# The 16-step loop of the two middle layers, written out with an order of work for each engine

## The reference, cut to what matters

```
def _layer(x, wqkv, qs, ksc, wo, lg, lb, w1, b1, w2, b2):
    h = shift_token(x)                      # second half of the channels comes from the token before
    q, k, v = split(h @ wqkv)               # 8 heads of 64
    q, k = rotary_xpos(l2norm(q) * qs, l2norm(k) * ksc)
    o = local_attention(q, k, v)            # windows of 128: own window and the one before, masked softmax
    x = x + o @ wo
    h = shift_token(x)
    h = (h - mean) / sqrt(var + 1e-5) * lg + lb
    a, g = split(h @ w1 + b1)               # 2 x 682
    return x + (a * gelu(g)) @ w2 + b2
```

## Time and profile before

| what | us |
|---|---|
| median of 3 runs | 3072.92 (3065.40 to 3076.16) |
| the profiled execution, time | 3070.95 |
| its span, first to last instruction | 3069.2 |
| PE busy in the span | 2724.8 (89%) |
| DVE busy | 2044.3 (67%) |
| ACT busy | 1430.0 (47%) |
| POOL busy | 1000.7 (33%) |

### The profile page before, as it was taken

One profiled execution on the slowest core, in us unless ns is written; L12 is line 12 of the kernel. 1 busy time (PEld: TensorE's weight loads), 2 busy tenths in 40 slices (PEclk: granted clock), 3 DMA queues, 4 the chain that ended last, 5 costly groups with the idle time before them and its releaser, 6 DMA issues. The chain is left out here.

```text
span 3069.2 us, 60378 instructions
## 1 busy us (share of the span) xinstructions
PE 2724.8 (89%) x20578; PEld 2415.7 (79%) x20578; DVE 2044.3 (67%) x5302; ACT 1430.0 (47%) x3028; POOL 1000.7 (33%) x906
## 2 busy tenths in 40 slices
PE   7999999958999999997799999999858899679997
PEld 6998898847888888886688888888847688577886
DVE  6777777637777777774577777777647355484554
ACT  5666676624555555553355555555426111062111
POOL 2222222224333333331343333333224333263332
PEclk8999999969999999998799999999979899889998
DMA  1011110022222222222222222222234101041100
GB/s 64 26 31 34 35 34 31 23 92 71 80 64 68 82 63 69 78 67 76 73 73 72 68 75 67 67 80 63 66 108 137 60 28 35 30 132 38 42 28 21
DMA packets 222985, 188.10 MB, mean 61 GB/s; under 512 B 22356, under 2 KB 204504, under 8 KB 221912
## 3 DMA queue, kind: packets, MB, share of 16 engines
q1 hardware_dynamic: 203224, 174.42, 17.7%
q10 hardware_dynamic: 19584, 11.35, 1.2%
HBM read 89.95 MB, written 44.04 MB: 44 GB/s over the span
## 5 line engine op out<-in xcount | busy, mean ns | idle before, releaser
L1292 ACT ACTIVATE b_sb_probs<-b_sb_probs,b_sb_neg_top,b_sb_r_norm 128x256 f32<-128x256 f32 x512 | 265.7, 590 | 155.4 <-DVE b_sb_neg_top L1400 154.4
L1212 POOL TENSOR_TENSOR b_sb_r_norm<-b_sb_squares,b_sb_power 128x8 f32<-128x8 f32 x64 | 105.0, 1641 | 705.6 <-DVE b_sb_squares L1359 705.6
L2166 ACT ACTIVATE c_sb_kern_hi<-c_sb_kern 128x512 fp32r<-128x512 f32 x128 | 80.8, 632 | 428.3 <-DVE c_sb_kern L2186 428.3
L2143 POOL TENSOR_TENSOR c_sb_kern_lo<-c_sb_kern,c_sb_kern_hi 128x512 fp32r<-128x512 f32 x128 | 166.7, 1303 | 312.9 <-ACT c_sb_kern_hi L2166 312.9
L118 PE MATMUL psum<-b_sb_fT_lo,b_sb_w_hi 128*128 128x256 f32 x768 | 229.6, 299 | 27.9 <-DVE b_sb_fT_lo L1462 27.9
L2182 DVE SCALAR_TENSOR_TENSOR c_sb_kern<-psum,cu_bias 128x512 f32<-128x512 f32 x128 | 88.4, 691 | 246.4 <-PE psum L120 246.3
L1393 DVE CUSTOM_DVE_ANT_0 b_sb_probs<-psum,b_sb_mask_now 128x256 f32<-128x256 f32 x512 | 196.6, 421 | 64.5 <-PE psum L1539 57.7
L120 PE MATMUL psum<-b_sb_fT_hi,b_sb_w_hi 128*128 128x256 f32 x768 | 218.5, 285 | 0.0
L119 PE MATMUL psum<-b_sb_fT_hi,b_sb_w_lo 128*128 128x256 f32 x768 | 217.8, 284 | 0.0
L1329 ACT ACTIVATE b_sb_gate<-psum,b_sb_b 128x256 f32<-128x256 f32 x192 | 90.6, 474 | 271.8 <-PE psum L120 271.7
L118 PE MATMUL psum<-c_sb_kern_lo,cu_v_hi 128*128 128x512 f32 x512 | 206.9, 404 | 2.9 <-POOL c_sb_kern_lo L2143 2.9
(11 more groups left out here) (309 smaller groups left out, 9014.1 us busy)
## 6 DMA issues: line engine op xcount, KB each, us to landing
b_sb_v_prev<-b_sb_v_now SPq DMA_DIRECT2D x64, 260.0 KB, 2.3
b_sb_kT_hi<-b_sb_kT_hi SPq DMA_DIRECT2D x64, 256.0 KB, 2.5
b_sb_kT_lo<-b_sb_kT_lo SPq DMA_DIRECT2D x64, 256.0 KB, 2.6
Y<-b_sb_y SPq DMA_DIRECT2D x128, 128.0 KB, 1.7
b_sb_res<-Y SPq DMA_DIRECT2D x64, 128.0 KB, 2.2
b_sb_h_in<-Y ACTq DMA_DIRECT2D x128, 64.0 KB, 1.8
b_sb_x_f<-Y SPq DMA_DIRECT2D x128, 64.0 KB, 1.9
b_sb_res_f<-Y SPq DMA_DIRECT2D x64, 128.0 KB, 2.1
```

Of the source, the lines that this page charges most:

```text
L1212: pool.tensor_tensor(r, s, p, ALU.pow).then_inc(r_ready[b], 1)
L1292: ins = act.activation(probs[b][:, n, :], probs[b][:, n, :], ACT.Exp, bias=neg_top[b][:, n:n + 1], scale=r_norm[b][:, h:h + 1])
L2143: pool.tensor_tensor(kern_lo[n][:], kern[n][:], kern_hi[n][:].bitcast(F32), ALU.subtract)\
```

## The change

The loop of `layer_b` is written out: `staggered`, `Chain`-based waits of the loop and `fence` go, `turns` and `in_turns` come in, as in layer a. Step numbers are then plain integers: all waits and addresses are constants. Its stages compute the same as before.

```
-    order = [("load", 1, 0), ("load_r", 0, -2), ("load_r", 1, -2), ("scores", 1, -1), ("residual", 1, -1),
-             ("project_k", 0, 0), ("scores2", 1, -1), ("turn_p", 1, -1), ("project_q", 0, 0), ("turn_p2", 1, -1),
-             ("turn_f", 0, -2), ("project_v", 0, 0), ("up", 0, -2), ("up", 1, -2), ("mid", 0, -2), ("values", 1, -1),
-             ("up", 2, -2), ("mid", 1, -2), ("turn_h", 1, 0), ("up", 3, -2), ("mid", 2, -2), ("turn_o", 1, -1),
-             ("up", 4, -2), ("mid", 3, -2), ("turn_qk", 0, 0), ("out", 1, -1), ("up", 5, -2), ("mid", 4, -2), ("mid", 5, -2),
-             ("load", 0, 1), ("load_f", 0, -1), ("load_f", 1, -1), ("scores", 0, 0), ("residual", 0, 0),
-             ("project_k", 1, 0), ("scores2", 0, 0), ("down", 0, -2), ("turn_p", 0, 0), ("project_q", 1, 0),
-             ("turn_p2", 0, 0), ("project_v", 1, 0), ("values", 0, 0), ("moments", 0, -1), ("down", 1, -2),
-             ("turn_o", 0, 0), ("norm", 0, -1), ("turn_h", 0, 1), ("turn_qk", 1, 0), ("rope", 0, 1), ("out", 0, 0)]
+    order = {
+        "act": [("turn_f", 0, -4), ("mid", 4, -5), ("project_v", 0, -2), ("turn_o", 1, -3), ("mid", 5, -5), ("up", 0, -4),
+               ("up", 1, -4), ("project_v", 1, -2), ("turn_h", 0, -1), ("load", 1, -1), ("turn_qk", 1, -2),
+               ("scores", 0, -2), ("mid", 0, -4), ("scores2", 0, -2), ("scores", 1, -2), ("mid", 1, -4), ("turn_p2", 0, -2),
+               ("project_k", 0, -1), ("scores2", 1, -2), ("up", 2, -4), ("turn_h", 1, -1), ("up", 3, -4),
+               ("project_q", 0, -1), ("mid", 2, -4), ("turn_p2", 1, -2), ("project_k", 1, -1), ("load", 0, 0), ("up", 4, -4),
+               ("mid", 3, -4), ("turn_o", 0, -2), ("up", 5, -4), ("turn_qk", 0, -1), ("project_q", 1, -1)],
+        "pe": [("scores", 0, -1), ("up", 0, -3), ("up", 1, -3), ("project_v", 1, -1), ("turn_h", 0, 0), ("turn_qk", 1, -1),
+               ("out", 1, -2), ("scores2", 0, -1), ("down", 0, -4), ("down", 1, -4), ("scores", 1, -1), ("turn_p", 0, -1),
+               ("up", 2, -3), ("scores2", 1, -1), ("turn_p2", 0, -1), ("project_k", 0, 0), ("values", 0, -1),
+               ("turn_p", 1, -1), ("up", 3, -3), ("turn_h", 1, 0), ("project_q", 0, 0), ("up", 4, -3), ("turn_p2", 1, -1),
+               ("project_k", 1, 0), ("turn_o", 0, -1), ("values", 1, -1), ("up", 5, -3), ("turn_qk", 0, 0),
+               ("project_q", 1, 0), ("turn_f", 0, -2), ("project_v", 0, 0), ("out", 0, -1), ("turn_o", 1, -1)],
+        "dve": [("up", 5, -4), ("turn_qk", 0, -1), ("turn_f", 0, -3), ("sums_q", 1, -1), ("spin_q", 1, -1), ("out", 0, -2),
+               ("mid", 4, -4), ("turn_o", 1, -2), ("scores", 0, -1), ("mid", 5, -4), ("up", 0, -3), ("turn_h", 0, 0),
+               ("up", 1, -3), ("turn_qk", 1, -1), ("out", 1, -2), ("scores2", 0, -1), ("down", 0, -4), ("scores", 1, -1),
+               ("turn_p", 0, -1), ("scores2", 1, -1), ("down", 1, -4), ("mid", 0, -3), ("moments", 0, -2), ("sums_k", 0, 0),
+               ("spin_k", 0, 0), ("up", 2, -3), ("values", 0, -1), ("turn_h", 1, 0), ("turn_p", 1, -1), ("sums_q", 0, 0),
+               ("spin_q", 0, 0), ("mid", 1, -3), ("sums_k", 1, 0), ("up", 3, -3), ("spin_k", 1, 0), ("norm", 0, -2),
+               ("mid", 2, -3), ("up", 4, -3), ("mid", 3, -3), ("turn_o", 0, -1), ("values", 1, -1)],
+        "sp": [("out", 1, -2), ("scores2", 0, -1), ("residual", 1, -1), ("rope", 0, 0), ("load_r", 0, -3),
+               ("residual", 0, -1), ("load_f", 0, -2), ("load_f", 1, -2), ("scores2", 1, -1), ("values", 1, -1),
+               ("load_r", 1, -3), ("values", 0, -1), ("down", 0, -4), ("down", 1, -4), ("out", 0, -1)],
+        "pool": [("moments", 0, -3), ("project_k", 0, -1), ("project_q", 0, -1), ("project_k", 1, -1), ("load_r", 0, -4),
+                ("project_q", 1, -1), ("rope", 0, 0)],
+    }
...
-        o_n = sb("o_n", [P, B_INNER])
+        o_n = [sb(f"o_n{b}", [P, B_INNER]) for b in both]
...
-        front = Banks(sem, psum, f"{name}_front", range(0, 3), [(job[:-1], int(job[-1])) for job in of_front])
-        back = Banks(sem, psum, f"{name}_back", range(3, 6), [(job, b) for b in both for job in of_back])
-        ffn = Banks(sem, psum, f"{name}_ffn", range(6, 8), ["f"] + [f"w{m}" for m in range(B_FC)] + ["y0", "y1"])
+        main = Ring(sem, psum, f"{name}_main", range(0, 6), [(t, (job, b)) for stage, t, b in turns(order["pe"], NT)
+                                                             if stage in jobs for job in jobs[stage]])
+        ffn = Ring(sem, psum, f"{name}_ffn", range(6, 8), [(t, (f_jobs[stage], b)) for stage, t, b in turns(order["pe"], NT)
+                                                           if stage in f_jobs])
...
             def turn_o(t, b):
-                back.wait_full(act, t, ("oT", b))
-                if b:
-                    back.wait_full(act, t, ("wo", b - 1))
-                else:
-                    back.wait_last_full(act, t, ("wo", BATCH - 1))
+                main.wait_full(act, t, ("oT", b))
+                main.wait_last_full(act, t, ("wo", b))
...
-            def turned_by(t, b, n, job, so_far):
+            def sums(t, b, n):
...
+            def spin(t, b, n, job):
...
             def scores2(t, b):
                 tops(t, b, (2, 3))
-                if b == BATCH - 1:
-                    own[b].link(dve.tensor_copy(mask_now[:], mask[:, 1, :]))
```

More of the change, by code:

```diff
@@ L120, in product3 @@
     return pe.matmul(out, w_hi, x_hi, start=False, stop=last)
[L123 to L142, removed]
 def turns(order, steps):
@@ L1109, in layer_b @@
         y2 = sb("y2", [P, BATCH, D])
-        front = Banks(sem, psum, f"{name}_front", range(0, 3), [(job[:-1], int(job[-1])) for job in of_front])
-        back = Banks(sem, psum, f"{name}_back", range(3, 6), [(job, b) for b in both for job in of_back])
-        ffn = Banks(sem, psum, f"{name}_ffn", range(6, 8), ["f"] + [f"w{m}" for m in range(B_FC)] + ["y0", "y1"])
+        jobs = {"turn_h": ["h"], "project_k": ["k"], "project_q": ["q"], "project_v": ["v"], "turn_qk": ["kT", "qT"],
+                "scores": ["s0", "s1"], "scores2": ["s2", "s3"], "turn_p": ["p0", "p1"], "turn_p2": ["p2", "p3"],
+                "values": ["o0", "o1"], "turn_o": ["oT"], "out": ["wo"]}
+        f_jobs = {"turn_f": "f", "up": "w", "down": "y"}
+        main = Ring(sem, psum, f"{name}_main", range(0, 6), [(t, (job, b)) for stage, t, b in turns(order["pe"], NT)
+                                                             if stage in jobs for job in jobs[stage]])
+        ffn = Ring(sem, psum, f"{name}_ffn", range(6, 8), [(t, (f_jobs[stage], b)) for stage, t, b in turns(order["pe"], NT)
+                                                           if stage in f_jobs])
         consts_ready, rope_loaded, rope_ready = (sem(f"{name}_{n}") for n in ("consts_ready", "rope_loaded", "rope_ready"))
@@ L1333, in mid_ @@
                 if m == 0:
-                    ffn.wait_last_full(act, t, "y1")
+                    ffn.wait_last_full(act, t, ("y", 1))
                 act.wait_ge(mid_ready, t * B_FC + m + 1)
                 act.activation(mid_hi[:, m, :], mid[m % 2][:], ACT.Copy).then_inc(mid_hi_ready, 1)
-            staggered(act, order, NT, {"load": load, "turn_h": turn_h, "project_k": project_k, "project_q": project_q,
+            in_turns(order["act"], NT, {"load": load, "turn_h": turn_h, "project_k": project_k, "project_q": project_q,
                                        "project_v": project_v, "turn_qk": turn_qk, "scores": scores, "scores2": scores2,
-                                       "turn_p2": turn_p2, "turn_o": turn_o, "turn_f": turn_f, "up": up, "mid": mid_}, [])
+                                       "turn_p2": turn_p2, "turn_o": turn_o, "turn_f": turn_f, "up": up, "mid": mid_})
         @block.vector
         def _(dve):
-            own_qk = [Chain(dve, dve_qk[b], 2) for b in both]
-            own = [Chain(dve, dve_own[b], 2 + b) for b in both]
-            own_f = Chain(dve, dve_ffn, 2)
+            own = Links(dve, dve_own)
             dve.wait_ge(consts_ready, 9)
@@ L1480, in down @@
             def down(t, b):
-                ffn.wait_full(dve, t, f"y{b}")
+                ffn.wait_full(dve, t, ("y", b))
                 dve.wait_ge(sum_ready, t + 1)
                 dve.wait_ge(y2_stored[b], 16 * t)
-                ffn.read(dve.tensor_tensor(y2[:, b, :], ffn.out(f"y{b}", D), sum_f[:, b, :], ALU.add), f"y{b}")
-            staggered(dve, order, NT, {"turn_h": turn_h, "project_q": project_q, "project_v": project_v, "turn_qk": turn_qk,
-                                       "scores": scores, "scores2": scores2, "turn_p": turn_p, "values": values, "turn_o": turn_o, "out": out,
+                ffn.read(t, dve.tensor_tensor(y2[:, b, :], ffn.out(t, ("y", b), D), sum_f[:, b, :], ALU.add), ("y", b))
+            in_turns(order["dve"], NT, {"turn_h": turn_h, "sums_k": sums_k, "spin_k": spin_k, "sums_q": sums_q, "spin_q": spin_q,
```

(5 more changed lines are left out.)

320 lines of the change are left out of this document (157 added, 163 removed).

## The result

The changed kernel takes 2920.99 us (median of 4 runs, 2915.55 to 2922.95), the kernel before 3071.7 beside it: ratio 0.951, 95% interval 0.949 to 0.953. I had forecast 3027, range 2990 to 3075: the direction was right, the gain over three times what I had (151 us, not 46).

What follows compares the result with a forecast made beforehand. PE was taken to bound the two middle loops, with only its waits to win: -28.1 us a layer in full passes and +5 at the ends, -46.2 in all, from 3070.95 to 3024.8, plus 1.97, say 3027; range 2990 to 3075.

Steps and rivals of the forecast that it cites:

- 43.7 us is the floor of a step: Steady step of the middle loops: PE's work stays the same, so no step can take less than 43.7 us.
- rival 3: Middle loops: all PE waits go and the ends cost nothing more, -37.7 us a layer, 2998; chance 0.12, cheaper ends included.
- 12 x 0.8 = 9.6 in place of 37.7 us: -28.1 us a layer: Full passes: PE's waits fall from 2.9 to 0.8 us a step, -28.1 us a layer.
- The three large waits: Steady step: PE's waits ahead of `up` 0 and `scores` (0.8 us each) and `turn_p` (0.5 us) go.
- the three places on the ring that I found tight: Ring of six banks: `project_q` 0, `project_k` 1 and `project_v` 0 need late drains, about 1 us to spare.
- Layer a's 1.4: PE's idle us a step in layer a, of the same form; upper end for the 0.8 us taken as left.
- I take +5 us a layer: Partly filled first and last passes of each middle loop: +5 us a layer, bounds -10 and +16.
- Writing out: Register arithmetic for waits and addresses goes, code grows: price 0, bounds -3 and +3 us a loop.
- Second buffers, 0: `o_n`, `oT` per batch and the mask without its copy: 0, no more than -0.3 us a step.
- Rival 1: Steady step: another wait takes the place, 2.4 us left a step, -3 us a layer, 3067, no change; chance 0.09.
- Rival 2: Full passes: the clock falls, a spell costing 3.3 us in each of 12, 3106, slower; chance 0.15.
- What would show it: Signs in the trace: rotary period 44.5 us, PE busy 43.7 a step, first full pass about 135 us after loop start.

## Why the prediction was wrong, step by step

- **"PE's jobs stay the same, so 43.7 us is the floor of a step."** This step failed. 43.73 is PE's busy time in a step, and it held 1.1 us of waiting: under the shown ends of matmuls, and in the late second product behind a wait. The changed kernel runs at 42.6, so the floor is that or less. The range stood on it: even rival 3, with no wait left, came to 2998.
- **"12 x 0.8 = 9.6 in place of 37.7 us: -28.1 us a layer."** Mis-sized. It is 12 x 3.97 = -47.6, 19.5 more. 12.6 of it is the 1.05 us a step that no row shows, 9.6 the 0.8 that I left. Against that I counted 13 turns of the hardware loop, which has 12 (the `Fori` runs from 3 to 15, and the earlier trace rows show 12 periods): 35.0 us and not 37.7. The three large waits went as walked, and the three places on the ring that I found tight held: 0.09 us of wait a step. Layer a's 1.4 was no guide.
- **"I take +5 us a layer"** for the ends. Wrong in sign. On my footing, a loop less 16 floors and less the excess of 12 full passes, the ends went from 776.5 - 682.1 - 47.6 = 46.8 to 17.5 us in loop 1 (-29.3), and from 40.7 to 18.9 in loop 2 (-21.8). 15.9 of each is my estimate for the four steps' worth of work in the partly filled passes, at the same 3.97 us; I had priced these waits as if only full passes had them. Most of what is left in loop 1 (13.4) is the clock: the last 99.9 us of it before had 0.91 and the first 69 us 0.90, that is up to 9.0 and 6.9 us lost (at half clock a us of work takes two); the changed kernel has 1.00 and 0.94, 0 and 4.1. In loop 2 (5.9 left) the last 47 us had 1.00 before and 0.96 after, and the first 69 us 0.90 and 0.94, so the clock explains about 1 us of it. That the passes are filled better, with less time in chains of single operations, is my reason for the rest; no run tested it.
- **Writing out, "price 0".** Right for the time; the steps got up to 0.35 us shorter by it, 4.3 and 2.9 us over 12 steps of the two loops. The jump back of the loop over the layers grew by 3.8 us, which I had not looked at.
- **Second buffers, 0**: right. That the mask's copy costs nothing by itself was not tried.
- **Rival 1** did not come, but two experiments show how near it was: the same rings with the old order, or the same orders with the old rings, put waits of 2.5 to 3.5 us in each step. **Rival 2** did not come: 1.00 in the steps, 0.99 over each loop. Regular waits alone did not lower the clock in the kernel before either: 1.00 over 12 steps with five or six waits in each, of 0.8 us and less. **Rival 3** was the right mechanism, all waits go; its 2998 came from the same false floor.
- **What would show it**: I wrote "PE busy in a step: still 43.7". It is 42.5 (382.74 / 9), and this line alone would have told floor from measurement. The period of the rotary table was forecast as 44.5 and is 42.63; the first full pass starts 133.2 us after the loop's start, near the 135 forecast.

The time came out 103 us under the forecast. The full passes hold 39 of it (2 x 19.5), the ends 61 (29.3 + 5 and 21.8 + 5), the gap and the stages around 3. The terms put right: two loops x 16 steps x 3.97 = -127.0, ends -13.4 and -5.9, gap +4.0, stages around -7.2, sum -149.5.

## What to carry to other kernels

Take the floor of a matmul-bound step from the distance between the starts of its products, not from the busy time of the engine: each wait of PE cost its row and about 0.2 us more here, up to 0.3, so many short waits are worth more to remove than they show. An order and the ring of buffers that it runs on are one design: try them together, since each alone can lose what both win. Before rewriting a list, try a single swap at its largest wait; here it gave 42.5 of 151 us. When an engine gets fewer columns to do and the kernel gets slower, look at what it now collides with.

## What the runs showed of the hardware

- A matmul of 512 columns is shown 0.40 us long and of 256 columns 0.28, at 0.23 and 0.12 us from start to start (clock 1.00); after a wait the first one of 256 columns holds the next 0.22 us off.
- A DVE operation with both inputs in SBUF, started while POOL worked, ended with POOL's operation: 8 columns in 1.14 us, not 0.15; 256 columns in 1.56, not 0.42, and 0.28 us behind POOL's end. A move of one POOL operation by some 9 us was worth 20 us of 2945.
- A jump back over a body of 16 written-out steps cost 4.4 us, with six instruction blocks fetched in it. The 12 turns of the hardware loop over one step fetched seven in all and cost at most 0.35 us each, registers and addresses included.
